# A fused perceiver block on one core: the self-attention's weighted sums as four 64 by 64 tiles, its kept rows on GpSimd

## The chip, the cores and the metric

The kernel runs on one core of a Trainium2 chip. The metric is the device time of one execution in microseconds (us). Before the change three runs gave 592.71, 593.39 and 594.58 us, median 593.39.

## The reference

Three residual blocks follow each other on `x` of shape (64, 32, 256): a cross-attention to a context, a causal self-attention along the first axis, and a mixture of eight experts of which two are used per token. Only the second one is touched by the change. Its part of the reference, cut to what matters:

```python
def _L0_attn_ref(inputs, W, proj, concat_w, concat_b):      # inputs: layernorm(x), (64, 32, 256)
    hp = jnp.tanh(jnp.einsum('sbh,hk->sbk', inputs, W))
    scores = jnp.einsum('sbk,k->sb', hp, proj)
    mask = t_idx[None, :] < t_idx[:, None]                  # strictly earlier positions
    logits = jnp.where(mask[:, :, None], scores[None, :, :], neg)
    attn = jax.nn.softmax(logits, axis=1)
    context = jnp.einsum('tsb,sbh->tbh', attn, inputs)
    cat = jnp.concatenate([inputs, context], axis=-1)
    out = jnp.tanh(jnp.einsum('tbc,hc->tbh', cat, concat_w) + concat_b)
    out = out.at[:2].set(inputs[:2])                        # the first two positions keep their input
    return out
x = x + _L0_attn_ref(_layernorm(x, axis=-1), ...)
x = x + _L0_ffn_ref(_layernorm(x, axis=-1), ...)
```

Since a weight row is applied to `inputs` and then multiplied by the second half of `concat_w`, the kernel multiplies first: it makes the values `inputs @ concat_w[:, 256:].T` plus the bias, and sums them with the attention weights.

## The kernel before

The 2048 tokens lie as 16 tiles of 128 rows by 256 columns in `xb`. One tile holds two of the 32 batch entries with 64 positions each, so its rows 0 to 63 and 64 to 127 belong to different sequences. The self-attention runs from 336.5 to about 411 us of the profiled execution, between the cross-attention and the experts, in four chunks `c` of four tiles. Each engine has a program of its own, a loop `for k in range(6)` written out by hand; step `k` handles chunk `k` at its entrance, chunk `k-1` in the middle, and chunk `k-2` (the normalisation and the gate of the experts) at the end. The engines meet only in semaphores. Banks of PSUM are dealt out in turn by the list `plan`, which says for every use which semaphore sets the bank free.

For one chunk the work is:

- TensorE: `hidden` (L1246), `turned` of the next chunk, `logits` (L1269, 64-column tiles side by side), `products` (L1280, the values), `direct` (L1293), then `lifted` for the chunk before, `crossed` (L1305: the 128 by 128 weights `Ab` of each tile transposed), `gated`, `mixed` (L1312) and `turned_back`. `mixed` adds the weighted sums to the banks `ay` that `direct` has begun. It is four matmuls, each 128 by 128 weights against 256 columns. Half of `Ab` is zero, since the two sequences of a tile don't see each other; GpSimd clears it once at the start and VectorE writes only the two blocks on the diagonal.
- VectorE, in order within a step: `third` of chunk `k-2` (L1515: `zs`, masked, added to `xb`, then the moments), `lowered` of chunk `k`, `masked` of chunk `k-1`, `kept` of chunk `k` (L1479: `xb` plus the normalised rows of the first two positions, one instruction over 128 by 1024), `final_norm` of chunk `k-2`, `weighted` of `k-1` (L1504: reciprocal, then two instructions that write `Ab`, rows 0 to 63 and rows 64 to 127), `values` of `k-1` (L1486: two instructions of 128 by 512 out of PSUM into `Yv`), then the routing work of the experts: `positions` and `marks` of `k-3`, `best` and `chosen` of `k-2`.
- ScalarE: `squashed`, `highs`, `exps` of `k-1` (L1703), `final_norm`, `normed` of `k+1` (L1669), `gate_in`, `weights` (L1711: the transposed weights out of PSUM into `AT`), `gate_out` and `outs` (L1724: tanh of `ay` into `zs`).
- GpSimd: only `scales` (L1647), four instructions of 128 by 4 that turn moments into the scale `rs` and the shift `nb` of a normalisation, for both normalisations. Step `k` does `scales(1, k-2)` and then `scales(0, k+2)`.
- SyncE loads expert weights and biases into space that comes free. The bias of expert 1 goes where `xn` lies, so it waits until `turned` and `kept` have read `xn` for the last time.

In step 5 there is no chunk left to hide behind: `third(3)` on VectorE, then `raised` (L1323) and `weighed` (L1333) on TensorE, `best` and `chosen_of_two` on VectorE, and `rank`.

Of the kernel before, what the change touches and what calls it, by code (L numbers as in the profile page):

```python
# [6 lines left out]
ALU = mybir.AluOpType  # L7
# [69 lines left out]
def build(nc, d, out, vx_d, w1_d, y_d, g_d):  # L77
    ctx = ExitStack()
    with ctx:
# [214 lines left out]
        pf = put("pf", [128, 2, NTILE])  # L294
        area(167, 199)
# [75 lines left out]
        for k in range(6):  # L371
# [9 lines left out]
            if 0 <= c < 4:  # L381
                plan += [(("Y", c, h), u_yb, 2 * c + h + 1) for h in range(2)]
# [16 lines left out]
        def bank(*key):  # L399
            return B[place[key] % 7]  # L400

# [174 lines left out]
        with nc.Block() as block:  # L576
# [593 lines left out]
            def _(sp):  # L1170
# [33 lines left out]
                sp.wait_ge(u_b2, 4)  # L1204
# [19 lines left out]
            def _(t):  # L1224
# [80 lines left out]
                def crossed(c):  # L1305
                    b = take("at", c)
                    t.wait_ge(u_a, 2 * c + 2)
                    for j in range(4):
                        mm = t.transpose(b[:, 128 * j:128 * j + 128], Ab[:, j, :], ident)
                    mm.then_inc(u_at, 1)  # L1310

                def mixed(c):  # L1312
                    t.wait_ge(u_ate, c + 1)
                    t.wait_ge(u_yb, 2 * c + 2)
                    for h in range(2):
                        b = bank("ay", c, h)
                        for jj in range(2):
                            j = 2 * h + jj
                            mm = t.matmul(b[:, C * jj:C * jj + C], AT[:, j, :], Yv[:, j, :],
                                          start=False, stop=(jj == 1), skip_group_check=True)  # L1320
                        mm.then_inc(u_o, 1)
# [107 lines left out]
            def _(v):  # L1429
# [49 lines left out]
                def kept(c):  # L1479
                    if c == 0:  # L1480
                        v.wait_ge(u_xv, 2)
                    v.wait_ge(u_xn, on_scalar(c))
                    v.scalar_tensor_tensor(out=xb[:, 4 * c:4 * c + 4, :], in0=xn[:, :, :], scalar=m10,
                                           in1=xb[:, 4 * c:4 * c + 4, :], op0=ALU.mult, op1=ALU.add).then_inc(u_b2, 1)

                def values(c):  # L1486
                    for h in range(2):
                        v.wait_ge(u_yp, 2 * c + h + 1)
                        if c:
                            v.wait_ge(u_o, 2 * c)  # L1490
                        v.tensor_tensor(Yv[:, 2 * h:2 * h + 2, :], bank("Y", c, h)[:, :].rearrange("p (a c) -> p a c", a=2),
                                        bcc[:, 1, :].unsqueeze(1).broadcast_to([128, 2, C]), ALU.add).then_inc(u_yb, 1)

                def masked(c):
                    v.wait_ge(u_sc, c + 1)
                    if c:
                        v.wait_ge(u_a, 2 * c)
# [6 lines left out]
                def weighted(c):  # L1504
# [5 lines left out]
                    for h in range(2):  # L1510
                        r = slice(64 * h, 64 * h + 64)
                        v.tensor_tensor(Ab[r, :, 64 * h:64 * h + 64], L[r, :, :],
                                        sm[r, 2, :].unsqueeze(2).broadcast_to([64, 4, 64]), ALU.mult).then_inc(u_a, 1)

                def third(c):  # L1515
                    v.wait_ge(u_b2, c + 1)
# [79 lines left out]
                for k in range(6):  # L1596
# [6 lines left out]
                    if k < 4:  # L1603
                        kept(k)
# [38 lines left out]
            def _(g):  # L1643
# [12 lines left out]

                scales(0, 0, u_mv, u_r, u_rs)
                scales(0, 1, u_mv, u_r, u_rs)
                for k in range(6):
                    if 0 <= k - 2 < 4:  # L1660
                        scales(1, k - 2, f_mv, f_r, f_rs)
                    if k + 2 < 4:
                        scales(0, k + 2, u_mv, u_r, u_rs)

            @block.scalar
            def _(a):
                a.wait_ge(s_ote, T)

                def normed(c):  # L1669
                    a.wait_ge(u_rs, c + 1)  # L1670
                    if c:
                        a.wait_ge(u_t, 2 * c)
                        a.wait_ge(u_b2, c)
# [29 lines left out]
                def exps(c):  # L1703
                    a.wait_ge(u_nm, c + 1)
                    if c:
                        a.wait_ge(u_a, 2 * c)
# [402 lines left out]
```

## Time and profile before

| what | value |
|---|---|
| median of three runs | 593.39 us |
| the profiled execution, its own time | 592.44 us |
| its span | 590.6 us |
| TensorE busy | 579.2 us, 98% |
| VectorE busy | 459.9 us, 78% |
| ScalarE busy | 350.9 us, 59% |
| GpSimd busy | 329.3 us, 56% |

The span runs from the first to the last instruction; the 1.8 us between it and the execution's own time lie outside. In the trace one fp32 matmul of TensorE is two records (two passes), so the four matmuls of `mixed` are eight. A transpose is one record. Lines of the form "start, length, engine, line, operation" are in microseconds from the start of the span.

### The profile page before, as it was taken

The page shows a single profiled execution, that of the slowest core. Times are in us where ns is not written, and L with a number is a line of the kernel's source. Part 1 is how long each engine was busy: PE and PEld are TensorE (multiplying, and loading weights), DVE is VectorE, ACT ScalarE, POOL GpSimd, SP SyncE. Part 2 cuts the span into 40 slices and gives each one's busy share as a digit, 9 for nine tenths or more (in the row PEclk, how much of TensorE's full clock was granted, in tenths as well). Part 3 has the DMA queues.
Part 4 walks back from the last instruction along what each step waited for, and adds up shares of the span by engine and source line. Part 5 has one row for each costly group of instructions (what it writes and reads, how often), then busy time and mean ns, then how long its engine had stood idle before and what let it go on. Part 6 is the DMA issues. An engine that isn't in the chain of part 4 may idle for free.

```text
span 590.6 us, 21921 instructions
## 1 busy us (share of the span) xinstructions
PE 579.2 (98%) x8431; PEld 479.8 (81%) x8431; DVE 459.9 (78%) x1064; ACT 350.9 (59%) x769; POOL 329.3 (56%) x481
## 2 busy tenths in 40 slices
PE   9999999999999999999999999999899999999997
PEld 4888878888788888788888788888478888887597
DVE  3688867888677887777777687698878888888496
ACT  4677867878777778677776444655433333333363
POOL 3456867878758788578887231011267666663000
PEclk9999999999999999999999999999899999999999
DMA  8625453676545745686430199535634334342895
GB/s 228 190 61 130 139 180 119 202 189 192 177 138 174 199 167 178 199 227 191 150 106 4 22 403 407 208 107 188 250 108 143 133 131 132 134 134 91 290 348 147
DMA packets 65399, 102.13 MB, mean 173 GB/s; under 512 B 15281, under 2 KB 41969, under 8 KB 64401
## 3 DMA queue, kind: packets, MB, share of 16 engines
q1 hardware_dynamic: 59200, 84.40, 45.2%
q0 software_dynamic: 4992, 15.34, 7.8%
q8 instruction: 70, 1.15, 0.8%
q10 hardware_dynamic: 1104, 0.99, 0.6%
q14 instruction: 33, 0.26, 0.2%
HBM read 69.43 MB, written 31.27 MB: 170 GB/s over the span
## 4 chain that ended last, share of the span: by engine, by line
PE 57%; POOL 20%; issue 14%; DVE 6%; DMA 1%; ACT 1%; POOLq 0%; SPq 0%; DVEq 0%
PE bank L2023 12%; PE scores L2023 6%; PE bank L1058 5%; PE bank L1065 5%; PE bank L1090 4%; POOL hA L732 4%; POOL lA L728 4%; PE bank L2051 4%; POOL hA L724 4%; PE scores L1106 3%; PE scores L1079 3%; PE scores L1242 2%; POOL Mb L765 2%; POOL tm L756 2%; PE bank L1017 2%
## 5 line engine op out<-in xcount | busy, mean ns | idle before, releaser
L864 DVE TENSOR_SCALAR Pm<-scores 128x514 f32<-128x514 f32 x128 | 88.1, 689 | 52.2 <-PE scores L1079 52.0
L980 ACT ACTIVATE Pm<-Pm,nm 128x257 f32<-128x257 f32 x256 | 115.7, 505 | 2.5 <-DVE nm L869 2.5
L869 DVE TENSOR_REDUCE nm<-Pm 128x2 f32<-128x514 f32 x128 | 87.5, 684 | 2.2
L975 ACT ACTIVATE PT<-bank 128x512 f32<-128x512 f32 x64 | 38.3, 598 | 74.1 <-PE bank L1090 74.1
L1058 PE MATMUL bank<-hA,wH 128*128 128x258 f32 x256 | 75.2, 305 | 0.1
L1090 PE MATMUL bank<-cst,Pm 128*128 128x128 f32 x512 | 70.0, 279 | 0.0
L1058 PE MATMUL bank<-hA,wL 128*128 128x258 f32 x256 | 69.3, 281 | 0.0
L1065 PE MATMUL bank<-wH,hA 128*128 128x256 f32 x256 | 68.9, 281 | 0.0
L1065 PE MATMUL bank<-wL,hA 128*128 128x256 f32 x256 | 68.8, 280 | 0.0
L2023 PE MATMUL bank<-W,xh 128*128 x208 | 66.6, 401 | 0.6 <-ACT xh L1943 0.6
L765 POOL TENSOR_TENSOR Mb<-Os,rc 128x64 f32<-128x64 f32 x64 | 21.7, 339 | 73.6 <-DVE rc L889 73.2
L1106 PEld LDWEIGHTS scores<-Vs,PT 128*32 128x32 f32 x4096 | 41.3, 110 | 25.9 <-issue 25.1
L1812 POOL DMA_INDIRECT g_d<-gg,ds x39 | 38.5, 987 | 35.4 <-DVE gg L1844 35.4
L1090 PEld LDWEIGHTS bank<-cst,Pm 128*128 128x128 f32 x512 | 54.8, 140 | 2.8 <-issue 0.8
L958 ACT ACTIVATE kT<-bank,bcol 128x258 f32<-128x258 f32 x128 | 53.7, 470 | 2.9 <-PE bank L1058 2.5
L1801 POOL DMA_INDIRECT Xg<-y_d,inv x39 | 38.0, 974 | 21.4 <-issue 11.3
L1058 PEld LDWEIGHTS bank<-hA,wH 128*128 128x128 f32 x256 | 48.4, 189 | 1.2 <-issue 1.1
L1058 PEld LDWEIGHTS bank<-hA,wL 128*128 128x128 f32 x256 | 48.5, 190 | 0.2 <-issue 0.2
L1106 PE MATMUL scores<-Vs,PT 128*32 128x17 f32 x4096 | 47.8, 186 | 0.7 <-issue 0.7
L1065 PEld LDWEIGHTS bank<-wH,hA 128*128 128x128 f32 x256 | 48.1, 188 | 0.0
L1065 PEld LDWEIGHTS bank<-wL,hA 128*128 128x128 f32 x256 | 48.1, 188 | 0.0
L1079 PE MATMUL scores<-kT,QF 32*64 32x258 f32 x1024 | 44.2, 402 | 0.6 <-POOL QF L742 0.6
(299 smaller groups left out, 1428.7 us busy)
## 6 DMA issues: line engine op xcount, KB each, us to landing
w_d<-whl SPq DMA_DIRECT2D x64, 256.0 KB, 3.2
W<-w_d SPq DMA_DIRECT2D x6, 2048.0 KB, 17.7
wst<-in_W1T SPq DMA_DIRECT2D x32, 256.0 KB, 3.7
cg<-g_d SPq DMA_DIRECT2D x16, 512.0 KB, 5.8
cx<-in_ctxT SPq DMA_DIRECT2D x31, 258.0 KB, 3.0
cx<-in_ctxT SPq DMA_DIRECT2D x62, 129.0 KB, 3.6
bb<-in_b SPq DMA_DIRECT2D x8, 512.0 KB, 6.0
W<-w_d SPq DMA_DIRECT2D x5, 512.0 KB, 5.2
```

The costliest lines, as they stand in the source:

```text
L864: v.tensor_scalar(Pm[:, i % 2, 2 * p:2 * p + 2, :], S4[:, 2 * p:2 * p + 2, 0:NK], -CLAMP, CLAMP, ALU.max, ALU.min).then_inc(s_cl, 1)
L869: v.tensor_reduce(nm[:, i % 2, 2 * p:2 * p + 2], Pm[:, i % 2, 2 * p:2 * p + 2, :], AX.X, ALU.max, negate=True).then_inc(s_nm, 1)
L958: a.activation(kT[:, i % 2, m, :], held("k", i, m)[:, 0:NKP], ACT.Identity, bias=bcol[:, 2 + m:3 + m]).then_inc(s_ke, 1)
L975: a.activation(PT[:, i % 2, 0, :, :].rearrange("p a b -> p (a b)"), held("p", i, 0)[:, :], ACT.Copy).then_inc(s_pte[0], 1)
L980: a.activation(Pm[:, i % 2, g, :], Pm[:, i % 2, g, :], ACT.Exp, bias=nm[:, i % 2, g:g + 1]).then_inc(s_ex, 1)
L1058: mm = t.matmul(b[:, 0:NKP], w[:, 128 * m:128 * m + 128], c, start=(e == 0), stop=(e == 4))
L1065: mm = t.matmul(b[:, C * c:C * c + C], x[:, 128 * c:128 * c + 128], w[:, C:2 * C], start=(e == 0), stop=(e == 4))
L1079: mm = t.matmul(B[g][64 * m:64 * m + 64, 0:NKP], QF[r, i % 2, m, :], kT[r, i % 2, m, :], start=True, stop=True, skip_group_check=True)
L1090: mm = t.transpose(b[:, o:o + 128], Pm[:, i % 2, 2 * p + gg, 128 * c:128 * c + 128], ident)
L1106: mm = t.matmul(pO[r, VH * g:VH * g + VH], PT[:, i % 2, p, 2 * gg + c, r], Vs[:, i % 4, c, 4 * (h // 2) + g, h % 2, :], start=first, stop= ...
L1812: g.indirect_dma_start(out=g_d, out_offset=bass.IndirectOffsetOnAxis(ap=ds[:, i:i + 1], axis=0), in_=gg[i % 3][:, :], in_offset=None).then ...
L2023: mm = t.matmul(o, x[:, i % 3, k, :], W1[:, bass.DynSlice(w + (part * 2048 + k * 1024 + 512 * h), 512)], start=(k == 0 and part == 0 and x ...
```

## The change

`mixed` becomes eight matmuls with 64 rows of weights and 64 output partitions each. For the first pair of tiles of a chunk (`h = 0`) they lie on the diagonal: rows 0 to 63 give partitions 0 to 63, rows 64 to 127 give partitions 64 to 127. For the second pair (`h = 1`) weights and values lie crosswise, so that rows 64 to 127 give partitions 0 to 63 and the other way round. Four of them, one for each quarter of the array, are issued one behind the other. To have the operands there, VectorE writes the blocks of `Ab` in four instructions of 64 by 128 in place of two of 64 by 256, and for `h = 1` writes `Yv` in two instructions of 64 by 512 that read one half of the partitions and write the other. `kept` leaves VectorE. GpSimd makes it out of `xb`, `rs` and `nb`, two instructions of 128 by 4 and four of 128 by 256 for each chunk, and no longer out of `xn`. ScalarE's `normed` and SyncE's load of a bias lose their wait for `kept`.

```diff
+        def half_of(h, r):
+            return slice(64 * (r ^ h), 64 * (r ^ h) + 64)
@@ SyncE
                 sp.wait_ge(u_t, 8)
-                sp.wait_ge(u_b2, 4)
                 load_bias(1)
@@ TensorE
                 def crossed(c):
-                    t.wait_ge(u_a, 2 * c + 2)
+                    t.wait_ge(u_a, 4 * c + 4)
                 def mixed(c):
                     t.wait_ge(u_ate, c + 1)
-                    t.wait_ge(u_yb, 2 * c + 2)
-                    for h in range(2):
-                        b = bank("ay", c, h)
-                        for jj in range(2):
+                    t.wait_ge(u_yb, 3 * c + 3)
+                    for jj in range(2):
+                        for h in range(2):
                             j = 2 * h + jj
-                            mm = t.matmul(b[:, C * jj:C * jj + C], AT[:, j, :], Yv[:, j, :],
-                                          start=False, stop=(jj == 1), skip_group_check=True)
-                        mm.then_inc(u_o, 1)
+                            for r in range(2):
+                                k, o = half_of(h, r), half_of(0, r)
+                                mm = t.matmul(bank("ay", c, h)[o, C * jj:C * jj + C], AT[k, j, o], Yv[k, j, :],
+                                              start=False, stop=(jj == 1), skip_group_check=True)
+                            if jj == 1:
+                                mm.then_inc(u_o, 1)
@@ VectorE
-                def kept(c):
-                    if c == 0:
-                        v.wait_ge(u_xv, 2)
-                    v.wait_ge(u_xn, on_scalar(c))
-                    v.scalar_tensor_tensor(out=xb[:, 4 * c:4 * c + 4, :], in0=xn[:, :, :], scalar=m10,
-                                           in1=xb[:, 4 * c:4 * c + 4, :], op0=ALU.mult, op1=ALU.add).then_inc(u_b2, 1)
                 def values(c):
-                        v.tensor_tensor(Yv[:, 2 * h:2 * h + 2, :], bank("Y", c, h)[:, :]..., bcc[:, 1, :]..., ALU.add)
+                        for r in (slice(0, 128),) if h == 0 else (slice(0, 64), slice(64, 128)):
+                            to = r if h == 0 else half_of(1, r.start // 64)
+                            v.tensor_tensor(Yv[to, 2 * h:2 * h + 2, :], bank("Y", c, h)[r, :]..., bcc[r, 1, :]..., ALU.add)
                 def weighted(c):
                     for h in range(2):
-                        r = slice(64 * h, 64 * h + 64)
-                        v.tensor_tensor(Ab[r, :, 64 * h:64 * h + 64], L[r, :, :], sm[r, 2, :]..., ALU.mult)
+                        for r in range(2):
+                            b = half_of(0, r)
+                            v.tensor_tensor(Ab[b, 2 * h:2 * h + 2, half_of(h, r)], L[b, 2 * h:2 * h + 2, :],
+                                            sm[b, 2, 2 * h:2 * h + 2]..., ALU.mult)
                 def third(c):
-                    v.wait_ge(u_b2, c + 1)
+                    v.wait_ge(u_b2, 6 * c + 6)
@@ GpSimd
+                def kept(c):
+                    k = slice(4 * c, 4 * c + 4)
+                    if c >= 2:
+                        g.wait_ge(u_b2, 6 * (c - 1))
+                    g.tensor_scalar(kf[:, c % 2, 0, :], rs[:, k], m10, 1.0, ALU.mult, ALU.add).then_inc(u_b2, 1)
+                    g.tensor_scalar(kf[:, c % 2, 1, :], nb[:, 0, k], m10, 1.0, ALU.mult, ALU.mult).then_inc(u_b2, 1)
+                    g.wait_ge(u_b2, 6 * c + 2)
+                    if c == 0:
+                        g.wait_ge(u_xv, 2)
+                    g.wait_ge(u_xn, on_scalar(c))
+                    for j in range(4):
+                        n = 4 * c + j
+                        g.tensor_scalar(xb[:, n, :], xb[:, n, :], kf[:, c % 2, 0, j:j + 1], kf[:, c % 2, 1, j:j + 1],
+                                        ALU.mult, ALU.add).then_inc(u_b2, 1)
                 for k in range(6):
                     if 0 <= k - 2 < 4:
                         scales(1, k - 2, f_mv, f_r, f_rs)
+                    if k < 4:
+                        kept(k)
                     if k + 2 < 4:
                         scales(0, k + 2, u_mv, u_r, u_rs)
@@ ScalarE
                 def normed(c):
                     if c:
                         a.wait_ge(u_t, 2 * c)
-                        a.wait_ge(u_b2, c)
```

The remaining waits on `u_a` and `u_yb` (`masked`, `exps`, the plan of banks) only follow the new counts.

## Rows read from the trace of the kernel before

**Rows 1.** The page: busy time, share of the span and instructions of each engine
```profile
PE 579.2 (98%) x8431; PEld 479.8 (81%) x8431; DVE 459.9 (78%) x1064; ACT 350.9 (59%) x769; POOL 329.3 (56%) x481
```

**Rows 2.** Windows, steps 3-4: length; busy PE, PEld, DVE, ACT, POOL; clock; DMA
```profile
380.60:395.60 15.00, 14.94 (x120) 12.72 (x120) 14.36 (x53) 7.21 (x21) 1.60 (x4) 1.00 0.24 72
395.60:411.20 15.60, 15.23 (x128) 12.60 (x126) 13.52 (x52) 8.22 (x21) 1.59 (x4) 1.00 0.51 172
```

**Rows 3.** The chain that ended last, in order of time: start, length, what
```profile
380.43 0.17 PE bank L1372
...
410.39 0.75 DVE xb L1520
...
411.28 0.63 PE bank L1330 x4
...
412.68 1.92 PE bank L1341 x16
```

**Rows 4.** Timeline of TensorE: `mixed(1)` and what follows it
```profile
378.09 1.13 PE L1319 MATMUL bank<-Yv,AT 128*128 128x256 f32 x4
...
379.93 0.51 PE L1370 MATMUL bank<-WgT,cst 128*128 128x8 f32 x4
```

**Rows 5.** Timeline of TensorE: matmuls on parts of the array, and their successors
```profile
299.97 0.69 PE L1079 MATMUL scores<-kT,QF 32*64 32x258 f32 x16
300.59 0.74 PE L1106 MATMUL scores<-Vs,PT 128*32 128x17 f32 x64
...
384.18 1.08 PE L1274 MATMUL scores<-hp,bcol 128*64 128x256 f32 x8
385.19 0.50 PE L1288 MATMUL scores<-WcR,xTh 128*128 128x256 f32 x2
```

**Rows 6.** Timeline of VectorE, steps 3 and 4, with idle time and its releaser
```profile
380.63 0.17 DVE L1541 COPY s<-bank 128x8 f32<-128x8 f32 x1 [5.00 <-PE bank L1372]
...
388.11 1.28 DVE L1483 SCALAR_TENSOR_TENSOR xb<-xn,cst,xb 128x1024 f32<-128x1024 f32 x1
389.31 0.73 DVE L1476 TENSOR_SCALAR yn<-xb,mv,rs 128x256 f32<-128x256 f32 x2
389.95 0.17 DVE L1506 RECIPROCAL sm<-sm 128x4 f32<-128x4 f32 x1
390.16 0.87 DVE L1512 TENSOR_TENSOR Ab<-L,sm 64x256 f32<-64x256 f32 x2
391.06 0.69 DVE L1491 TENSOR_TENSOR Yv<-scores,bcc 128x512 f32<-128x512 f32 x1
...
392.27 0.21 DVE L456 TENSOR_TENSOR pr<-oh,bank 128x64 f32<-128x64 f32 x1
...
404.00 0.18 DVE L1506 RECIPROCAL sm<-sm 128x4 f32<-128x4 f32 x1 [1.50 <-ACT L L1708]
...
422.81 0.29 DVE L1633 TENSOR_TENSOR tb<-th,c 128x128 f32<-128x128 f32 x1
```

**Rows 7.** Timeline of ScalarE: `normed(2)`, and the last instruction of `exps(2)`
```profile
357.33 2.06 ACT L1676 ACTIVATE xn<-xb,nb,rs 128x256 f32<-128x256 f32 x4
...
389.49 0.19 ACT L1708 ACTIVATION_READ_ACCUMULATOR L<-L,sm 128x1 f32 x1
```

**Rows 8.** Timeline of GpSimd: three instructions of `scales`
```profile
348.33 1.06 POOL L1653 TENSOR_SCALAR nb<-mv 128x4 f32<-128x4 f32 x1
...
354.09 0.20 POOL L1653 TENSOR_SCALAR nb<-mv 128x4 f32<-128x4 f32 x1
...
387.88 0.20 POOL L1655 TENSOR_TENSOR nb<-nb,rs 128x4 f32<-128x4 f32 x1
```

**Rows 9.** Costliest groups of GpSimd: busy us, mean ns of one, idle before
```profile
L724 POOL TENSOR_SCALAR hA<-cx 128x516 fp32r<-128x516 f32 x60 | 37.4, 624 | 0.0
```

**Rows 10.** What SyncE's queue waited for: total us, times, longest
```profile
SPq L1204 <- DVE xb L1483: 15.1, 1, 15.1
```

**Rows 11.** A window of step 5, columns as in rows 2
```profile
416.00:418.00 2.00, 1.18 (x17) 0.97 (x18) 1.41 (x8) 1.33 (x3) 0.00 (x0) 0.59 0.54 213
```

More of the change, by code:

```diff
@@ L294, in build @@
         pf = put("pf", [128, 2, NTILE])
+        kf = put("kf", [128, 2, 2, 4])
         area(167, 199)
@@ L381, in build @@
             if 0 <= c < 4:
-                plan += [(("Y", c, h), u_yb, 2 * c + h + 1) for h in range(2)]
+                plan += [(("Y", c, h), u_yb, 3 * c + 2 * h + 1) for h in range(2)]
             if 0 <= k - 3 < 2:
@@ L1490, in values @@
                             v.wait_ge(u_o, 2 * c)
-                        v.tensor_tensor(Yv[:, 2 * h:2 * h + 2, :], bank("Y", c, h)[:, :].rearrange("p (a c) -> p a c", a=2),
-                                        bcc[:, 1, :].unsqueeze(1).broadcast_to([128, 2, C]), ALU.add).then_inc(u_yb, 1)
+                        for r in (slice(0, 128),) if h == 0 else (slice(0, 64), slice(64, 128)):
+                            to = r if h == 0 else half_of(1, r.start // 64)
+                            v.tensor_tensor(Yv[to, 2 * h:2 * h + 2, :],
+                                            bank("Y", c, h)[r, :].rearrange("p (a c) -> p a c", a=2),
+                                            bcc[r, 1, :].unsqueeze(1).broadcast_to([r.stop - r.start, 2, C]), ALU.add
+                                            ).then_inc(u_yb, 1)
                 def masked(c):
@@ L1496, in masked @@
                     if c:
-                        v.wait_ge(u_a, 2 * c)
+                        v.wait_ge(u_a, 4 * c)
                     v.tensor_tensor(L[:, :, :], bank("s", c)[:, 0:256].rearrange("p (j s) -> p j s", s=64),
@@ L1510, in weighted @@
                     for h in range(2):
-                        r = slice(64 * h, 64 * h + 64)
-                        v.tensor_tensor(Ab[r, :, 64 * h:64 * h + 64], L[r, :, :],
-                                        sm[r, 2, :].unsqueeze(2).broadcast_to([64, 4, 64]), ALU.mult).then_inc(u_a, 1)
+                        for r in range(2):
+                            b = half_of(0, r)
+                            v.tensor_tensor(Ab[b, 2 * h:2 * h + 2, half_of(h, r)], L[b, 2 * h:2 * h + 2, :],
+                                            sm[b, 2, 2 * h:2 * h + 2].unsqueeze(2).broadcast_to([64, 2, 64]), ALU.mult
+                                            ).then_inc(u_a, 1)
                 def third(c):
-                    v.wait_ge(u_b2, c + 1)
+                    v.wait_ge(u_b2, 6 * c + 6)
                     for h in range(2):
@@ L1602, in _ @@
                         masked(k - 1)
-                    if k < 4:
-                        kept(k)
                     if k == 5:
@@ L1705, in exps @@
                     if c:
-                        a.wait_ge(u_a, 2 * c)
+                        a.wait_ge(u_a, 4 * c)
                     for j in range(4):
```

## The prediction

> **What bounds the kernel now.** The page comes first: TensorE is busy in 98% of the span [rows 1], so a reader would take it for the bound everywhere and book every saved matmul as time saved. The windows of steps 3 and 4 correct that. From 380.6 to 395.6 us TensorE is busy 14.94 of 15.00 us, and VectorE 14.36; in the next stretch it is 15.23 and 13.52 of 15.60 [rows 2]. Two engines are full side by side, and only the chain tells which one sets the end. Read in order of time it leaves TensorE after `turned_back(0)` at 380.6, and it comes back at 411.28, with `raised` [rows 3]. Between them it is on VectorE, but for the wait for `exps(3)`. The timeline of VectorE confirms it: before 380.63 it has been idle 5.00 us, waiting for TensorE; behind that its only long wait is the 1.50 us before the reciprocal at 404.00 [rows 6]. So chunks 0 and 1 are set by TensorE and have room on VectorE; chunks 2 and 3 are set by VectorE, and `third(3)` at 410.39 [rows 3] is what the rest of the kernel stands behind. Everything below is the sum of what reaches that one start.
>
> **TensorE: `mixed`.** It now takes from 378.09 to 379.93, 1.84 us to the start of its successor [rows 4]: eight passes, one behind the other. After the change there are two rounds of four tiles and two passes each. Four tiles of 64 by 64 are not in the trace. The nearest rows are `logits`, two rounds of two tiles with the same 256 columns, 384.18 to 385.19, 1.01 us, and the scores of the cross-attention, one round of eight tiles of 32 by 64, 299.97 to 300.59, 0.62 us [rows 5]. The number of tiles in a round costs next to nothing there, the number of rounds does. I take 1.01 us, a saving of 0.83 us for each chunk. The bounds are 0 (the tiles run one after the other) and half of 1.84, 0.92. `mixed(0)` and `mixed(1)` lie ahead of the handover at 380.63, so that moves 2 x 0.83 = 1.66 us earlier. `mixed(2)` and `mixed(3)` save as much, but while VectorE is behind: nothing.
>
> **VectorE: `kept` goes.** In chunk 3's turn (step 3) it takes 388.11 to 389.31, 1.20 us to its successor [rows 6]. What is late next is `exps(2)`: its last instruction ends at 389.49 + 0.19 = 389.68 [rows 7], and the reciprocal starts 0.03 later at the earliest, against 389.95 now. The gain is 389.95 - 389.71 = 0.24 us, not 1.20. In steps 0 to 2 VectorE waits for TensorE anyway and the removal is worth nothing, and steps 4 and 5 have no `kept`.
>
> **VectorE: `weighted` is cut in four.** Now two instructions of 64 by 256 take 0.87 us together, and the next starts 0.90 after the first; two instructions of 128 by 256 that stay on the same partitions, in `final_norm`, take 0.73 [rows 6]. An instruction that starts on other partitions than the one before it therefore doesn't overlap it, while the others overlap by 0.09. An instruction of 128 elements is 0.29 long (L1633) [rows 6]. The four new ones change partitions each time: 4 x (0.29 + 0.03) = 1.28 against 0.90, +0.38 us. If they did overlap it would be 4 x 0.20 = 0.80, -0.10.
>
> **VectorE: `values` becomes three.** Two instructions now take 391.06 to 392.27, 1.21 us, at 0.61 each with the overlap, 0.69 one by itself [rows 6]. Half the partitions save no time, since time goes by the elements of one partition. Three at 0.61 make 1.83, +0.62; three without overlap make 3 x (0.69 + 0.03) = 2.16, +0.95. Each starts on other partitions than its predecessor on one of its sides, so I take +0.95, by the row of `weighted`. The Trainium skill speaks against this part of the change (VectorE: DVE Perf Modes, section "Two Vector instructions with no wait between them"): an instruction is held until all earlier ones have finished when its first input or its output starts in another group of 32 partitions than the last one did. By that rule all three and the one behind them are held, +0.95; the trace shows it for inputs and outputs that move together [rows 6], not for an output that moves alone, and without that half of the rule the first crosswise instruction would overlap and the term would be 0.11 smaller.
>
> Per chunk that is +1.33 us (bounds +0.52 and +1.33), and it counts twice, for chunks 2 and 3. In chunks 0 and 1 the 5.00 us of idle time before 380.63 [rows 6] hide it; if that cover were gone it would cost 1.33 each.
>
> **GpSimd.** `kept(3)` stands behind `scales(1, 1)`, which ends at 387.88 + 0.20 = 388.08 [rows 8], then 1.66 earlier, 386.42. Two small instructions at 0.20 [rows 8] with a wait make some 0.6 us. One of 128 by 256 lies between 0.20 for 4 columns [rows 8] and 0.62 for 516 [rows 9], by a straight line 0.41, four make 1.6: the end is at 388.7. `third(3)` needs it at 411, `scales(1, 2)` stands behind it and isn't due before 401: hidden. `scales(0, 2)` and `scales(0, 3)` now stand behind `kept(0)` and `kept(1)`, some 2.2 us each. The first was through at about 354.5 (one more of 0.20 behind the row at 354.09 [rows 8]), and ScalarE reads it in `normed(2)` from 357.33 [rows 7]: 2.8 us to spare, so even a full 2.2 would be hidden. ScalarE reads the second a whole step later. What isn't hidden: the two engines can hold each other up. GpSimd's instruction of 4 columns took 1.06 us at 348.33 beside VectorE's `kept`, against 0.20 at 354.09 [rows 8]. The new `weighted(2)` starts at 390.16 - 1.66 - 0.24 = 388.26, in the last of the four. It costs between 0 and one such instruction, 0.41; I take 0.20.
>
> **SyncE and ScalarE.** SyncE's wait of 15.1 us for `kept` before a bias load [rows 10] goes. The load starts earlier, what stands behind it in the queue waits for `yn` and `mixed` all the same, and nobody needs the bias before the experts: 0. `normed` loses a wait for an instruction that no longer exists: 0, since TensorE isn't idle there.
>
> **The sum.** -1.66 - 0.24 + 2 x 1.33 + 0.20 = +0.96 us at `third(3)`. Behind it the work is the same. The profiled execution took 592.44 us, 0.95 below the median; 593.40 would be its sum, and on the median of 593.39 it is 594.35. I forecast 594.3: what TensorE gives, VectorE takes.
>
> **Rivals.**
>
> *The clock (slower).* Now TensorE is granted its full clock, 1.00, through steps 3 and 4 [rows 2], and falls to 0.59 in the mean of 416 to 418 [rows 11], between its levels of 2.4 and 1.2 GHz, after a stretch of thin matmuls and waits. The change gives TensorE 4 x 0.83 = 3.3 us less to do ahead of a `third(3)` that comes 0.96 later: some 4.3 us more of waiting in step 4, much of it before `lifted(2)` and behind `mixed(3)`. The clock can then fall before `raised` and `weighed`. These stand in the chain with 0.63 [rows 3] for a half of `raised` and 1.92 for `weighed` [rows 3], and at 1.2 GHz both double: between 0.6 and 2.5 us, taken as 1.6. It decides if the fall comes before about 414. For it: the fall is near already. Against it: `slots(1)` still lies in the gap. 594.35 + 1.6 = 595.9. Chance 0.2.
>
> *The tiles don't run side by side.* Then the 1.66 is missing: +2.62, 596.0. The Trainium skill has such a rule (TensorEngine Tiling (Array Packing), section "Restrictions and Gotchas", Gotcha 1): different row tiles cannot use the same PSUM bank at the same time. Here both row halves write to one bank, on different partitions. No row here shows that; the scores give each row group a bank of its own. Chance 0.1.
>
> *VectorE is cheaper than I think:* overlaps as now, no collision with GpSimd. -1.66 - 0.24 + 2 x 0.52 = -0.86, 592.5. The pair in `weighted` speaks against it. Chance 0.12.
>
> *TensorE sets the pace throughout,* as its 98% [rows 1] suggest. Then all four chunks count, -3.32, 590.1. The 30 us of the chain on VectorE speak against it. Chance 0.05.
>
> The forecast keeps 0.5 and 0.03 is left for the rest. About 0.3%, 1.8 us, is what a measurement can tell from no change. Faster by more (below 591.6) is the last rival and a tail: 0.07. Slower by more (above 595.2) is most of the first two and a tail: 0.30. Within: 0.63. The range is 592.3 to 596.3: from the cheap VectorE to the two slow rivals; what is left out is the last rival and the worst of the clock.
>
> **What would show it.** `mixed` at 1.0 us to its successor; the copy `s` of `best(0)` near 379.0; the reciprocal right behind `exps(2)`; from the first `Ab` to the first `Yv` 1.28, from there to `pr` 2.16; `third(3)` near 411.3 with `zs(3)` long done; TensorE idle for some 4 us in step 4; the granted clock still 1.00 at 411 to 415. I am wrong if VectorE shows waits between 379 and 411, or if `mixed` stays at 1.8.

## The result, and the profile after

The changed kernel takes 596.27 us (median of 20 runs, 594.97 to 598.67) against 593.38 us for the kernel before (20 runs beside them). The ratio is 1.0047, 95% interval 1.0036 to 1.0057: 2.9 us slower, and clear of no change. The profiled execution of the changed kernel took 596.94 us.

The page of the changed kernel, its first lines, as in [rows 1]:

```profile
span 595.1 us, 22019 instructions
...
PE 580.4 (98%) x8463; PEld 478.6 (80%) x8463; DVE 460.5 (77%) x1072; ACT 350.6 (59%) x769; POOL 339.8 (57%) x505
```

These shares tell little. The span grew by 4.5 us (it was 590.6) while TensorE's busy time grew by 1.2. The windows of steps 3 and 4 tell more (columns as in [rows 2]), with those of step 5 under them:

```profile
380.60:395.60 15.00, 14.01 (x128) 11.58 (x127) 13.45 (x43) 7.66 (x20) 4.36 (x10) 1.00 0.23 73
395.60:411.20 15.60, 13.62 (x125) 10.58 (x124) 13.37 (x53) 7.54 (x20) 1.62 (x4) 1.00 0.57 175
...
412.00:414.00 2.00, 1.48 (x8) 1.25 (x9) 2.00 (x5) 0.00 (x0) 0.00 (x0) 0.59 0.96 395
414.00:416.00 2.00, 2.00 (x10) 1.70 (x10) 1.97 (x18) 1.19 (x2) 0.61 (x2) 0.50 0.99 404
416.00:418.00 2.00, 2.00 (x11) 2.00 (x11) 0.35 (x4) 0.89 (x2) 0.99 (x3) 0.50 0.33 135
```

TensorE fell from 14.94 and 15.23 us busy [rows 2] to 14.01 and 13.62. Counted from the handover, the copy `s`, to the start of `raised`, it is idle for 3.91 us of 33.64 (windows 379.48:413.12), where before it was idle for 0.51 of 30.65 (380.63:411.28): 3.4 us of new idle time, and nothing came of it. And its granted clock is 0.59 in the mean of 412 to 414 and 0.50 from there on, 1.2 in place of 2.4 GHz. In the kernel before it was 1.00 until 416:

```profile
412.00:414.00 2.00, 1.89 (x16) 1.68 (x17) 1.97 (x17) 1.14 (x2) 0.46 (x2) 1.00 0.90 373
414.00:416.00 2.00, 1.57 (x8) 0.74 (x7) 1.72 (x21) 0.75 (x2) 1.13 (x3) 1.00 0.97 383
```

The timeline of VectorE (start, length, engine, line, operation; idle time in brackets), the lines that answer to [rows 6]:

```profile
336.51 0.28 DVE L898 STREAM_TRANSPOSE OT<-Mb 128x64 f32<-128x64 f32 x1 [0.28 <-POOL Mb L770]
...
379.48 0.17 DVE L1546 COPY s<-bank 128x8 f32<-128x8 f32 x1 [3.15 <-PE bank L1378]
...
388.55 0.18 DVE L1509 RECIPROCAL sm<-sm 128x4 f32<-128x4 f32 x1 [0.85 <-ACT L L1728]
388.76 1.82 DVE L1516 TENSOR_TENSOR Ab<-L,sm 64x128 f32<-64x128 f32 x4
390.61 0.69 DVE L1492 TENSOR_TENSOR Yv<-scores,bcc 128x512 f32<-128x512 f32 x1
391.34 1.41 DVE L1492 TENSOR_TENSOR Yv<-bank,bcc 64x512 f32<-64x512 f32 x2
392.77 0.22 DVE L461 TENSOR_TENSOR pr<-oh,bank 128x64 f32<-128x64 f32 x1
...
404.72 1.24 DVE L1516 TENSOR_TENSOR Ab<-L,sm 64x128 f32<-64x128 f32 x4
405.99 2.13 DVE L1492 TENSOR_TENSOR Yv<-scores,bcc 128x512 f32<-128x512 f32 x3
...
412.23 1.41 DVE L1525 SCALAR_TENSOR_TENSOR xb<-zs,cst,xb 128x512 f32<-128x512 f32 x2
...
418.65 0.19 DVE L1541 TENSOR_TENSOR gl<-bank,um 128x32 f32<-128x32 f32 x1 [2.30 <-PE bank L1347]
```

The copy `s` of `best(0)`, where VectorE takes over the chain, starts 1.15 us earlier (379.48 against 380.63 [rows 6]). In the trace of before, the last transpose of the cross-attention stood at 336.24, here it stands at 336.51, so the part before the change was 0.27 longer in this execution and the stage itself hands over 1.42 us earlier. From the copy to `third(3)` it takes 412.23 - 379.48 = 32.75 us; before it was 410.39 - 380.63 = 29.76 [rows 3, 6]. That is 2.99 more, and `third(3)` comes 1.84 later. From `third(3)` to the subtraction `gl` of `best(3)`, which waits for `weighed`, it takes 6.42 us; before it took 4.32, from the second of these lines of its VectorE timeline (the first is the transpose named above):

```profile
336.24 0.28 DVE L893 STREAM_TRANSPOSE OT<-Mb 128x64 f32<-128x64 f32 x1 [0.29 <-POOL Mb L765]
...
414.71 0.19 DVE L1536 TENSOR_TENSOR gl<-bank,um 128x32 f32<-128x32 f32 x1 [0.21 <-PE bank L1341]
```

That is 2.10 more. So the account of the profiled execution is 0.27 ahead of the stage, -1.42 at the handover, +2.99 on VectorE, +2.10 in step 5, and 0.56 behind it that I have not traced: 4.5 us.

TensorE's timeline of the changed kernel: `mixed(1)` (its first line) with its successor, the two halves of `slots(1)` (L453) with the waits before them, `raised` (L1336) and `weighed` (L1347).

```profile
377.65 0.43 PE L1324 MATMUL bank<-Yv,AT 64*64 64x256 f32 x2
...
378.67 0.61 PE L1376 MATMUL bank<-WgT,cst 128*128 128x8 f32 x4
...
411.17 0.40 PE L453 MATMUL bank<-A,Bv 128*128 128x128 f16 x4 [1.07 <-DVE A L514]
412.37 0.61 PE L453 MATMUL bank<-A,Bv 128*128 128x128 f16 x4 [0.81 <-DVE A L514]
413.12 1.94 PE L1336 MATMUL bank<-cst,xb 128*128 128x128 f32 x8
414.99 3.55 PE L1347 MATMUL bank<-WgT,gh 128*128 128x8 f32 x16
```

`mixed(1)` takes 1.02 us to its successor, in place of 1.84 [rows 4]: the four tiles do run side by side. `weighed` takes 3.55 in place of 1.92 [rows 3], and `raised` 1.94 in place of 1.29 (411.28 on the timeline of before).

`mixed(0)` saves less. These are its first line and the second line of `hidden` behind it, before and then changed:

```profile
363.41 1.13 PE L1319 MATMUL scores<-Yv,AT 128*128 128x256 f32 x4 [0.69 <-ACT AT L1715]
...
365.70 0.40 PE L1254 MATMUL bank<-xTl,WaR 128*128 128x512 f32 x1
```

```profile
363.67 0.43 PE L1324 MATMUL scores<-Yv,AT 64*64 64x256 f32 x2 [0.69 <-ACT AT L1735]
...
365.27 0.39 PE L1258 MATMUL bank<-xTl,WaR 128*128 128x512 f32 x1
```

That is 2.29 us before and 1.60 after, 0.69 less. From the start of `mixed(1)` to the copy `s` it is 2.54 us before (378.09 to 380.63 [rows 4, 6]) and 1.83 after (377.65 to 379.48), 0.71 less. Together they are 1.40 of the 1.42 us by which the handover comes earlier.

And GpSimd's `kept(3)`, which lies over VectorE's `weighted(2)` at 388.76:

```profile
387.61 2.20 POOL L1673 TENSOR_SCALAR xb<-xb,kf 128x256 f32<-128x256 f32 x4
```

### The profile page after: what moved, and what is told of

Read it like the earlier page. It is cut to its first block, busy times and chain, and to the rows that moved or that the text cites. A ratio compares the mean times of both kernels' runs of the same rounds, so it can differ in the third digit from the quotient of the medians.

```text
span 595.1 us, 22019 instructions
## 1 busy us (share of the span) xinstructions
PE 580.4 (98%) x8463; PEld 478.6 (80%) x8463; DVE 460.5 (77%) x1072; ACT 350.6 (59%) x769; POOL 339.8 (57%) x505
## 3 DMA queue, kind: packets, MB, share of 16 engines
q8 instruction: 70, 1.15, 0.8%
## 4 chain that ended last, share of the span: by engine, by line
PE 55%; POOL 20%; issue 14%; DVE 7%; DMA 2%; ACT 1%; POOLq 0%; SPq 0%; DVEq 0%; ACTq 0%
PE bank L2043 12%; PE scores L2043 6%; PE bank L1063 5%; PE bank L1070 5%; PE bank L1095 4%; POOL hA L737 4%; POOL lA L733 4%; POOL hA L729 4%; PE bank L2071 4%; PE scores L1111 3%; PE scores L1084 3%; PE scores L1246 2%; POOL Mb L770 2%; POOL tm L761 2%; PE scores L2019 1%
```

## The experiments

My theory after the result had three parts. VectorE pays more for the crosswise operands than TensorE saves ahead of the handover. GpSimd's `kept(3)` blocks VectorE's `weighted(2)`. The idle time that TensorE now has before `raised` lets its clock fall early. The rivals stand in each expectation. Every run is measured by two stretches of its VectorE timeline, since both leave out what lies ahead of the stage: A, from the copy `s` of `best(0)` to `third(3)`, and B, from `third(3)` to the subtraction `gl` of `best(3)`.

| kernel | copy `s` | `third(3)` | A | B | ratio to before, 95% interval |
|---|---|---|---|---|---|
| before | 380.63 | 410.39 | 29.76 | 4.32 | |
| changed | 379.48 | 412.23 | 32.75 | 6.42 | 1.0047 (1.0036 to 1.0057) |
| e1 filler | 379.79 | 412.54 | 32.75 | 4.33 | 1.0031 (1.0016 to 1.0045) |
| e2 kept early | 380.58 | 412.78 | 32.20 | 6.38 | 1.0040 (1.0026 to 1.0054) |
| e3 kept alone | 380.23 | 410.41 | 30.18 | 4.58 | 0.9998 (0.9976 to 1.0021) |
| e4 kept back | 379.65 | 412.32 | 32.67 | 6.06 | 1.0053 (1.0032 to 1.0073) |
| e5 two for Ab | 378.70 | 410.74 | 32.04 | 5.55 | 1.0036 (1.0013 to 1.0060) |
| e6 values straight | 378.60 | 409.45 | 30.85 | 5.05 | 1.0001 (0.9972 to 1.0030) |
| e7 mended | 378.83 | 410.04 | 31.21 | 4.32 | 1.0003 (0.9984 to 1.0022) |
| e8 mended, values straight | 378.89 | 408.27 | 29.38 | 4.33 | 0.9973 (0.9954 to 0.9993) |
| e9 values on ScalarE | 379.71 | 409.54 | 29.83 | 4.84 | 0.9990 (0.9965 to 1.0016) |
| e10 changed again | 379.90 | 412.65 | 32.75 | 5.62 | 1.0039 (1.0013 to 1.0065) |
| e11 filler again | 379.57 | 412.31 | 32.74 | 4.33 | 1.0003 (0.9980 to 1.0025) |
| e12 e9 without filler | 381.04 | 410.12 | 29.08 | 4.74 | 0.9982 (0.9966 to 0.9999) |

Runs e5 to e11 were on chips on which the kernel before takes 606 to 607 us; only ratios are compared across them. Of the runs below, e6 and e8 leave something out: their second half of the weighted sums is not the reference's. They price a step and are no kernels to use.

### e1 and e11: filler where TensorE waits

```diff
             for k in range(2):                      # in slots(t, c)
+                if c == 1:
+                    for o in range(0, (512, 384)[k], 128):
+                        t.matmul(pI[:, 128:256], cst[:, C_ONE:C_ONE + 128], cst[:, 0:128], start=False, ...)
                 t.wait_ge(u_ab, 2 * c + k + 1)
```

> The changed kernel with filler matmuls on TensorE where it now waits in step 4 and 5: four of 128 columns (about 0.86 us) ahead of slots(1) and three (about 0.65 us) between its two halves; nobody reads what they write. Theory (half of the loss is the clock): in the changed kernel third(3) starts 1.84 us later than before, but the gate's product ends 3.94 us later, because the granted clock is 0.5 from 412.35 on, 4 us earlier than before. With the waits of 1.07 and 0.81 us filled, the clock keeps 1.00 through raised and weighed, raised takes 1.3 us and weighed 1.9, and the ratio to the kernel before falls from 1.0047 to about 1.002 (some 1 to 2 us less). Rival (the clock falls in idle time that is there anyway and costs nothing; all of the loss is VectorE's): raised and weighed still end 1.84 us later at least and the ratio stays at 1.0047 within 0.001. Second rival (the clock falls for the thin matmuls of weighed, whatever is ahead of them): the fall stays at 412 to 413.

Measured: TensorE's windows, then `raised` and `weighed` on its timeline.

```profile
412.00:414.00 2.00, 1.56 (x14) 1.05 (x12) 2.00 (x5) 0.00 (x0) 0.00 (x0) 1.00 0.96 365
414.00:416.00 2.00, 1.85 (x16) 1.61 (x15) 1.97 (x15) 1.19 (x2) 0.30 (x2) 1.00 0.98 399
416.00:418.00 2.00, 1.72 (x9) 0.89 (x8) 1.75 (x23) 0.59 (x2) 1.29 (x3) 0.96 0.54 219
...
413.43 1.29 PE L1341 MATMUL bank<-cst,xb 128*128 128x128 f32 x8 [0.35 <-DVE xb L1530]
414.84 1.92 PE L1352 MATMUL bank<-WgT,gh 128*128 128x8 f32 x16
```

VectorE's stretch A is what it was to 0.01 us. The clock stays at 1.00 until nearly 418, `raised` and `weighed` take 1.29 and 1.92 us again, and B is 4.33, as before the change. The rival that the clock costs nothing is out for this stretch, since B is on the chain, and so is the one that `weighed` brings the fall about whatever is ahead of it. The mean granted clock of each execution says that the profile is no exception. It was 0.991 or less in 14 of the changed kernel's 20 executions, in 3 of the 32 of the kernel before that ran beside e1, and in none of the 12 with filler. The time fell by 0.9 us (596.27 to 595.34), less than the 2.1 of the profiled execution. The fall doesn't cost every execution the same: in the profiled one of e10, the same kernel, the clock is still 1.00 in the window 412:414 and 0.83 in 414:416, `raised` takes its 1.29 us, `weighed` 3.21, and B is 5.62 and not 6.42. The two intervals of the ratios overlap, so I ran both once more side by side:

> The changed kernel once more, on the same chip as the next one, to compare their times and mean granted clocks directly. Both theories: ratio to the kernel before 1.0047 within 0.001; by the theory of the clock, about 14 of 20 executions again have a mean clock of 0.991 or less, where the kernel before mostly has 0.994 or more.

> The changed kernel with the filler matmuls once more, beside the one before it on the same chip. Theory (the clock): 0.8 to 1.6 us faster than the changed kernel, nearly all executions at a mean clock of 0.994 or more. Rival (the clock costs nothing): equal within 0.3 us.

The changed kernel took 608.49 us and the one with filler 606.97 on one chip, 1.5 us apart. The ratios were 1.0039 and 1.0003. Their intervals overlap again, but both contain the noise of the same executions of the kernel before. Compared with each other, by resampling their 12 and 12 executions, the two kernels are 0.4 to 2.7 us apart (95%), so the filler's gain is clear of zero. The clocks didn't come out as written. A mean of 0.991 or less occurs in 5 of the changed kernel's 12 executions, 2 of 12 with filler and 5 of 29 of the kernel before; at 0.992 or less it is 10, 4 and 16. In this group the mean clock doesn't set the changed kernel apart from the one before, and falls elsewhere can enter it: in the profiled execution of e9, of the same group, it is 0.67 in the mean of 570 to 575 us. I hold 0.9 to 1.5 us for the clock's share in the median, by the times of both pairs and the mechanism in the profiles; 2.1 is shown for one profiled execution, and 1.3 for the other (B 5.62 against 4.32 or 4.33).

### e2: kept early

```diff
                 for k in range(6):                  # GpSimd
+                    if k < 4:
+                        kept(k)
                     if 0 <= k - 2 < 4:
                         scales(1, k - 2, f_mv, f_r, f_rs)
-                    if k < 4:
-                        kept(k)
```

> The changed kernel, but GpSimd does kept(k) ahead of scales(1, k-2), so kept(3) runs at 375 to 378 us, while VectorE waits for TensorE, and not beside weighted(2). Theory (the two engines block each other): the four instructions of weighted(2), which took 1.82 us in the changed kernel against 1.24 for weighted(3), take 1.24; third(3) comes 0.58 us earlier than in the changed kernel; ratio lower by about 0.001. Rival (weighted(2) is long for another reason, such as the order of its operands): it stays at 1.82, ratio unchanged.

```profile
389.87 1.24 DVE L1516 TENSOR_TENSOR Ab<-L,sm 64x128 f32<-64x128 f32 x4
391.14 0.69 DVE L1492 TENSOR_TENSOR Yv<-scores,bcc 128x512 f32<-128x512 f32 x1
```

The four instructions of `weighted(2)` take 1.24, as those of `weighted(3)`, and A is 0.55 shorter. The block is real and costs 0.58 us. The ratio, 1.0040 for 1.0047, fell by less than the intervals can tell.

### e3: kept alone on GpSimd, nothing else of the change

The edit is the diff of `kept` from the change, on the kernel before.

> The kernel before with kept on GpSimd and nothing else of the change. Theory: VectorE's reciprocal of chunk 2 comes 0.24 us earlier, as soon as exps(2) ends; weighted(2), now two instructions of 64 by 256, is blocked by GpSimd's four of 128 by 256 and loses up to 0.55 us; third(3) starts between 0.24 earlier and 0.3 later than before, and the time is within 0.5 us of the kernel before (ratio 0.999 to 1.001). Rival (taking 4 x 1.2 us off a busy VectorE shortens the kernel): 1 to 2 us faster, ratio 0.997.

```profile
389.30 0.18 DVE L1499 RECIPROCAL sm<-sm 128x4 f32<-128x4 f32 x1 [0.86 <-ACT L L1716]
389.51 1.44 DVE L1505 TENSOR_TENSOR Ab<-L,sm 64x256 f32<-64x256 f32 x2
390.98 0.69 DVE L1484 TENSOR_TENSOR Yv<-scores,bcc 128x512 f32<-128x512 f32 x1
```

The reciprocal comes 389.30 - 380.23 = 9.07 us behind the copy, 0.25 less than before, and then waits 0.86 for `exps(2)`: of the 1.20 us that left VectorE only the 0.25 counts. From the first `Ab` to the first `Yv` it is 1.47 in place of 0.90. Moving `kept` by itself costs A 0.42, a little more than the 0.3 that I had allowed, and changes the time by nothing measurable (593.92 against 593.83).

### e4: kept back on VectorE, the tiles alone

> The changed kernel with kept back on VectorE as it was, so only the tiles and their crosswise operands are left. Theory: kept costs 1.20 us of step 3, of which 0.95 fall into the wait for exps(2), so +0.25; the block of weighted(2) by GpSimd goes, -0.58. third(3) comes 0.3 us earlier than in the changed kernel, and the ratio stays within 0.001 of 1.0047. Rival (moving kept off VectorE is what keeps the loss small): 1.2 us or more slower than the changed kernel, ratio above 1.0065.

A was 32.67, 0.08 less than in the changed kernel and not 0.3. Reciprocal and `weighted(2)` did as expected, +0.25 and -0.58. But 0.28 us were lost between the reciprocal of chunk 3 and its first `Ab`, for which I have no reason. The ratio, 1.0053, is the same within its interval. That interval (to 1.0073) doesn't exclude the rival (above 1.0065) by itself; A does, since it is not 1.2 us longer. Together e3 and e4 say that the move of `kept` hardly matters either way: the loss comes with the tiles, by their operands on VectorE and by the clock.

### e5: Ab in two instructions, laid crosswise all the same

```diff
-                    for h in range(2):
-                        for r in range(2):
-                            ...                     # four of 64 by 128
+                    for r in range(2):
+                        b = half_of(0, r)
+                        a = Ab[b, :, :]
+                        to = bass.AP(tensor=a.tensor, offset=a.offset + 64 * r,
+                                     ap=[list(a.ap[0]), [256 + 64 - 128 * r, 2], [128, 2], [1, 64]])
+                        v.tensor_tensor(to, L[b, ...], sm[b, 2, ...], ALU.mult).then_inc(u_a, 1)
```

> The changed kernel, with the crosswise blocks of Ab written by two instructions of 64 by 256 (the output steps from one pair of tiles to the other by 320 or 192 columns) in place of four of 64 by 128. Theory (time goes by instructions and by their change of partitions, not by the crosswise layout): from the first Ab to the first Yv 0.90 us in chunk 3, as in the kernel before, against 1.27; in chunk 2 about 1.47, since GpSimd's kept(3) still blocks it, as in the run of kept alone; from best(0)'s copy to third(3) 32.0 us against 32.75. Rival (an output with three steps is slower): 1.2 or more in chunk 3.

```profile
403.60 0.87 DVE L1518 TENSOR_TENSOR Ab<-L,sm 64x256 f32<-64x256 f32 x2
404.50 2.13 DVE L1492 TENSOR_TENSOR Yv<-scores,bcc 128x512 f32<-128x512 f32 x3
```

0.90 us in chunk 3 and 1.48 in chunk 2, A 32.04: both terms as written. The layout of `Ab` costs nothing, the number of instructions does.

### e6: the values straight

The values of the second pair of tiles are written by one instruction of 128 by 512, not crosswise, as in the kernel before. TensorE does all its matmuls, on values that are not the right ones for the crosswise weights.

> The changed kernel with the values of the second pair of tiles laid straight, by one instruction of 128 by 512, so they aren't where the crosswise weights need them (the second half of the weighted sums is wrong; all instructions of TensorE are there). Theory: three held instructions at 0.72 are the largest part of VectorE's loss; from the first Yv to pr 1.21 us against 2.16, twice, third(3) 1.9 us earlier, 30.85 us behind best(0)'s copy, and the ratio to the kernel before 1.001 or less, with TensorE's clock falling late more often, since there is less idle time ahead of raised. Rival (another engine is right behind VectorE): third(3) gains less than 1.2 us because it waits for zs.

```profile
389.73 0.69 DVE L1490 TENSOR_TENSOR Yv<-scores,bcc 128x512 f32<-128x512 f32 x1
390.34 0.68 DVE L1490 TENSOR_TENSOR Yv<-bank,bcc 128x512 f32<-128x512 f32 x1
390.94 0.21 DVE L461 TENSOR_TENSOR pr<-oh,bank 128x64 f32<-128x64 f32 x1
```

1.21 us from the first `Yv` to `pr`, A 30.85 to the hundredth, ratio 1.0001. Twice 0.95 us, the largest term, is shown by taking it away.

### e7 and e8: all mended, and the same with the values straight

e7 joins e1, e2 and e5 and writes rows 64 to 127 of `Ab` first, so that the second `Ab` and the first `Yv` start on the same partitions. e8 adds e6, and leaves out the same as e6.

> All of the change, mended: kept early on GpSimd, Ab in two instructions with rows 64 to 127 first, the filler matmuls. Theory: the second Ab starts on the same partitions as the first Yv, which then overlaps it: 0.78 us from the first Ab to the first Yv, in both chunks, against 1.85 and 1.27 in the changed kernel. From best(0)'s copy to third(3) 31.2 us, and with the copy 1.4 us earlier third(3) is level with the kernel before: ratio 0.999 to 1.001. Rival (the order of the two plays no part): 0.90, third(3) 0.24 later. Rival (the clock falls early all the same): ratio 1.002 or more.

> The one before this with the values laid straight as well (the second half of the weighted sums is wrong), so the four tiles side by side cost VectorE next to nothing. Theory (TensorE's saving ahead of the handover passes through in full once VectorE doesn't pay for it): third(3) about 29.3 us behind best(0)'s copy, 1.9 us earlier than in the kernel before, ratio 0.9968. Rival (the saving is lost anyway, by the wait for exps, zs or yn): ratio 0.999 or more.

```profile
388.11 0.87 DVE L1523 TENSOR_TENSOR Ab<-L,sm 64x256 f32<-64x256 f32 x2
388.91 0.68 DVE L1497 TENSOR_TENSOR Yv<-scores,bcc 128x512 f32<-128x512 f32 x1
389.61 1.41 DVE L1497 TENSOR_TENSOR Yv<-bank,bcc 64x512 f32<-64x512 f32 x2
391.06 0.22 DVE L466 TENSOR_TENSOR pr<-oh,bank 128x64 f32<-128x64 f32 x1
```

In e7 the first `Yv` starts 0.80 us behind the first `Ab` and overlaps the second one, where it took 0.90 with the other order; that is worth 0.1 us by this pair. A is 31.21 and B 4.32. The kernel is level with the one before, 1.0003. That is as the parts add up: A is still 1.45 us longer than before, mostly the 2 x 0.95 of the values, and the handover comes 1.42 earlier. In e8, where only the values' crosswise layout is left out as well, A is 29.38 and the ratio 0.9973. TensorE's saving ahead of the handover does pass through in this kernel, where VectorE doesn't pay for it.

### e9 and e12: the crosswise values on ScalarE

e9 is e7 with this added; the bias of the crosswise values goes ahead of `direct` as a matmul.

```diff
+                def valued(c):                      # ScalarE, behind normed(k + 1)
+                    a.wait_ge(u_yp, 2 * c + 2)
+                    if c:
+                        a.wait_ge(u_o, 2 * c)
+                    for r in range(2):
+                        a.activation(Yv[half_of(1, r), 2:4, :], bank("Y", c, 1)[half_of(0, r), :]..., ACT.Copy)
                 def direct(c):                      # TensorE; bm holds the bias in two parts
+                        if h == 1:
+                            t.matmul(b[:, :]..., bo, bm...broadcast_to([..., 2, C]), start=True, ...)
```

> The mended kernel, and the two crosswise halves of the values go to ScalarE, as plain copies out of PSUM behind normed. Their bias goes ahead of direct as one matmul of TensorE per chunk (64 rows of ones against the bias in two parts, 512 columns, about 0.23 us), which is the same sum since the attention weights of a row add up to one. VectorE keeps one instruction of 128 by 512 per chunk. Theory (VectorE's 380 to 411 us are what counts, and ScalarE has room): from the first Yv to pr about 0.7 us against 2.16, best(0)'s copy 0.4 us later than in the mended kernel for the bias matmuls, from the copy to third(3) 28.4 us or, if zs comes last there, up to 29; third(3) 2.2 to 2.9 us earlier than in the kernel before, ratio 0.995 to 0.9965. Rival (ScalarE is right behind: the two copies delay exps, the gate's inputs or zs): from the copy to third(3) above 30 us, ratio 0.999 or more.

```profile
395.60:411.20 15.60, 15.54 (x149) 12.81 (x148) 12.09 (x40) 8.73 (x22) 1.61 (x4) 1.00 0.59 186
...
409.54 1.42 DVE L1538 SCALAR_TENSOR_TENSOR xb<-zs,cst,xb 128x512 f32<-128x512 f32 x2 [1.50 <-ACT zs L1776]
...
403.50 0.50 PE L1310 MATMUL bank<-bm,bo 64*128 64x512 f32 x1
403.93 0.50 PE L1318 MATMUL bank<-WcR,xTh 128*128 128x256 f32 x2
```

A miss: the ratio is 0.9990, no difference that can be measured. VectorE is 1.50 us ahead of `zs` now and TensorE is busy 15.54 of 15.60 us. I had priced the bias matmul at 0.23 us and it cost 0.43 to its successor, over 64 rows (403.50 to 403.93). The filler now stood in TensorE's way: `raised` starts with no wait, 1.43 us behind `third(3)`, where it was 0.89 in the kernel before. The bound had moved. e12 takes the filler out and lays the bias over all 128 rows, both at once, so it doesn't tell their shares apart.

> The kernel with ScalarE's values again, without the filler matmuls and with the bias matmul over all 128 rows. In the run before it TensorE was busy 15.54 of the 15.60 us of step 4: it had become the bound, the fillers stood in its way ahead of raised, and each bias matmul of 64 rows cost 0.43 us to its successor. Theory (TensorE is the bound there now): the bias matmul falls to about 0.25, zs(3) and with it third(3) come some 0.8 us earlier, 29.0 us or more behind best(0)'s copy, raised 1.0 to 1.5 us earlier, and the ratio is 0.996 to 0.998, the first version that beats the kernel before. Rival (without filler the clock falls before raised and takes the gain back): weighed takes 2.5 us or more, ratio 0.998 to 1.0.

```profile
404.34 0.40 PE L1305 MATMUL bank<-bm,bo 128*128 128x512 f32 x1
404.57 0.40 PE L1313 MATMUL bank<-WcR,xTh 128*128 128x256 f32 x2
...
410.12 1.42 DVE L1533 SCALAR_TENSOR_TENSOR xb<-zs,cst,xb 128x512 f32<-128x512 f32 x2 [0.90 <-ACT zs L1771]
...
412.42 2.33 PE L1356 MATMUL bank<-WgT,gh 128*128 128x8 f32 x16
```

The bias matmul costs 0.23, A is 29.08, and the time is 593.06 against 594.11 us, ratio 0.9982 with an interval that just leaves out 1. It is the only kernel here with the reference's whole computation that beats the one before, by 1.1 us or 0.2%, on 12 executions that were not repeated. The ratio lies a little above the 0.996 to 0.998 that I had written. Some of the gain went to the clock again: `weighed` took 2.33, which is most of the way to the rival's 2.5.

## Why the prediction was right, and where it was off

The forecast was 594.3 us with a range of 592.3 to 596.3. The measured 596.27 lies in the range by 0.03 us, on the side to which I gave 0.30 against 0.63 for no change. What it reached is the case of the first rival, 595.9, and not the forecast's own. The account of VectorE's own instructions was right; that the time stayed inside the range was luck. Two things were missing from the sum and they add: 0.61 us at `third(3)` and 0.9 to 1.5 behind it. With 594.35 they make 595.9 to 596.5, and the range ended at 596.3. Of the signs that I had named, the clock (still 1.00 at 411 to 415) is the one that failed. Step by step:

- *What bounds the kernel.* Right. A stretch of 30 us on VectorE stands between TensorE's handover and the rest, and in the runs up to e8 `third(3)` moved with VectorE's instructions, to 0.1 us of what was written beforehand in e2 and e5 to e8, while e3 and e4 missed it by 0.1 and 0.2. Only in e9 and e12, where VectorE had less to do, did it wait for `zs`. The rival that TensorE sets the pace throughout, -3.3 us, is out: TensorE got 3.4 us of idle time.
- *`mixed`.* 1.02 us against 1.01 written. The trace shows both row halves writing to one bank, on different partitions, without a delay. By this the Trainium skill's rule that different row tiles can't access one PSUM bank at once (TensorEngine Tiling (Array Packing), section "Restrictions and Gotchas") is not borne out for tiles that write to different partitions. But the handover came 1.42 us earlier, not 1.66. From the start of the successor of `mixed(1)` to the copy `s` it was 0.81 us (378.67 to 379.48), and 0.70 before (379.93 to 380.63 [rows 4, 6]), a tenth that I had left out; whether it is the switch to other tiles and back, no run tells. And `mixed(0)`, which I took for the same, took 1.64 us to its successor before (363.41 to 365.05) and not 1.84, and 1.03 after. With what stands right behind them the two save 0.69 and 0.71 and not 0.83 each, all but 0.02 of the 1.42.
- *`kept` off VectorE.* -0.24 written, -0.25 measured in the changed kernel (9.07 for 9.32 from the copy to the reciprocal) and in e3.
- *`weighted` in four.* +0.38 written; +0.37 in chunk 3 (1.27 for 0.90). e5 and e7 show the reason, instructions that change partitions.
- *`values` in three.* +0.95 written, +0.95 measured in both chunks, and e6 takes it away. The first crosswise instruction keeps its input's partitions and moves only its output, and it is held all the same: 390.61 to 391.34 is 0.73 us, the full length and no overlap. So the trace agrees with the half of the Trainium skill's rule that no row of before could show (VectorE: DVE Perf Modes, section "Two Vector instructions with no wait between them"). The instruction behind the last crosswise one, `pr`, shows it for inputs alone: its output begins at partition 0 like the one before, its inputs at 0 after inputs at 64. It starts 2.16 us behind the first `Yv` (390.61 to 392.77), 3 x 0.72, so it doesn't overlap either, as it did in the kernel before (2 x 0.61).
- *GpSimd against VectorE.* The term that was mis-sized. I wrote 0.20 with 0.41 as the most; it was 0.58 (1.85 to the first `Yv` against 1.27 in chunk 3), e2 removes it and e3 has 0.57 of it by itself. Two steps failed. One instruction of 128 by 256 took 0.55 us and not the 0.41 of the straight line, and `kept(3)` lasted until 389.81, not 388.7. So it lies over `weighted(2)` for 1.05 us (from 388.76) and not for 0.44 (from 388.26), and met two of VectorE's instructions and not one.
- *The sum at `third(3)`.* +0.96 written, +1.57 within the stage (1.84 less the 0.27 ahead of it). Of the 0.61 that was missing, 0.24 is the handover and 0.38 the block.
- *Behind it "the work is the same".* The step that failed, since it put this term at nothing. The work is the same and its clock isn't. It stood among the rivals, with the right place, the right cause and 1.6 us for a price; 2.1 in the profiled execution, 0.9 to 1.5 in the medians. But it had a chance of 0.2, when the 4.3 us of new idle time (3.4 measured) were a consequence of my own sum. A result that frees an engine right before a stretch where that engine is alone on the chain should have carried that cost in its own sum.

## What to carry to other kernels

An engine that is 98% busy is not therefore the bound: where another engine holds the chain, time saved on the first turns into waiting, and what the second pays for that saving comes through whole. Only what is saved ahead of the handover counts, here two of four chunks. On VectorE half the partitions save nothing (two instructions of 64 by 512 took 1.41 us, one of 128 by 512 took 0.69), and an instruction that starts on other partitions than the last one, on its input or its output alone, gives up its overlap of about 0.1 us. And look at what TensorE does right after the idle time you give it. If it is alone on the chain there, keep it busy until then; but where it has no waits, filler only stands in its way (e9).

## What the runs showed of the hardware that I had not expected

- Whether the clock falls in a stretch depended on what TensorE did ahead of it. With the same `raised` and `weighed` the clock was 1.00 through both in e1 and e11. Without filler it was 0.50 in the changed kernel's profiled execution, and in that of e10 it fell during `weighed`. The difference was filler of 8 and 6 passes of 128 columns in waits of 1.07 and 0.81 us.
- `weighed`, 16 passes of 8 columns, takes 1.92 us at the high level and 3.55 at the low one, although almost no columns go through: one of its weight loads took 0.19 us in the kernel before and 0.33 in the changed one (medians of 16).
- A matmul of 512 columns over 64 rows between others over 128 rows cost 0.43 us to its successor in e9, the same over 128 rows 0.23 in e12.
- GpSimd's `kept` of 128 by 256 with a scale and a shift per partition took 0.55 us, hardly less than 0.62 for a product with a constant over 516 columns [rows 9]. It is not VectorE's doing: in e2, where `kept(3)` runs while VectorE mostly waits, the four take 2.18 us, against 2.20.
